# A vision block's last stage: the sum with z moves from VectorE to TensorE

## The reference, cut to what matters

```python
h = _L0_tok_ref(x, ...)
h = h + _L0_attn_ref(_layernorm(h, axis=-1), ...)
h = h + _L0_ffn_ref(_layernorm(h, axis=-1), ...)
...
def _L0_ffn_ref(x, ...):
    ...
    moe_out = jnp.einsum('bseh,bse->bsh', expert_out, sparse)
    return _layer_norm(x + moe_out, gamma, beta)
```

## Time and profile before

| | us |
|---|---|
| median of 3 runs | 2013.91 |
| lowest and highest run | 2012.23, 2017.13 |
| profiled execution: its own time | 2015.43 |
| profiled execution: span | 2013.5 |
| PE busy | 1491.8 (74%) |
| PE weight loads (PEld) | 986.3 (49%) |
| DVE busy | 1425.9 (71%) |
| ACT busy | 1361.4 (68%) |
| POOL busy | 1095.7 (54%) |

### The profile page before, as it was taken

How to read it: one execution, slowest core, us unless ns; L and a number is a source line. 1 busy time by engine, 2 the same in 40 slices (tenths; PEclk the granted TensorE clock), 3 DMA queues, 4 the chain that set the end, 5 groups by cost and what they waited for, 6 DMA issues and landing times. The chain is left out here.

```text
span 2013.5 us, 49200 instructions
## 1 busy us (share of the span) xinstructions
PE 1491.8 (74%) x12152; PEld 986.3 (49%) x12153; DVE 1425.9 (71%) x3598; ACT 1361.4 (68%) x3957; POOL 1095.7 (54%) x1852
## 2 busy tenths in 40 slices
PE   6999957856656565664488885888882999995664
PEld 5999954421111111111244443445441988885563
DVE  2554559977777777786466666788886777675798
ACT  1333324419999999999599995777662776665675
POOL 2333330036666666664355553477775788887454
PEclk9999988965555555555555555555555999998887
DMA  7664410002222222221544543544533555554995
GB/s 297 251 244 175 183 40 1 1 25 81 87 76 85 76 75 76 79 93 55 120 137 137 149 147 116 167 154 152 153 131 111 138 139 142 139 147 115 296 288 155
DMA packets 184973, 263.31 MB, mean 131 GB/s; under 512 B 28372, under 2 KB 147363, under 8 KB 180328
## 3 DMA queue, kind: packets, MB, share of 16 engines
q1 hardware_dynamic: 137456, 202.16, 32.1%
q0 software_dynamic: 19840, 39.17, 5.5%
q10 hardware_dynamic: 27540, 20.52, 3.3%
HBM read 149.17 MB, written 108.01 MB: 128 GB/s over the span
## 5 line engine op out<-in xcount | busy, mean ns | idle before, releaser
L956 ACT ACTIVATE exps_summed<-s,neg_shift 128x197 f32<-128x197 f32 x1184 | 481.9, 535 | 32.1 <-POOL neg_shift L830 30.1
L956 ACT ACTIVATION_READ_ACCUMULATOR exps_summed<-s,neg_shift (+1 forms) x1184 | 339.2, 317 | 0.0
L993 DVE TENSOR_REDUCE score_max<-s 128x788 f32 (+3 forms) x320 | 285.9, 893 | 66.5 <-PE s L900 58.8
L1353 ACT ACTIVATE exps<-st,scalars 128x788 f32<-128x788 f32 (+1 forms) x320 | 246.4, 892 | 17.1 <-PE st L1262 17.1
L2034 POOL DMA_INDIRECT expert_sums<-y_tile,row_places x216 | 218.2, 1010 | 60.5 <-issue 28.6
L384 PE MATMUL mm<-w_tok,x_transposed 128*128 128x192 f32 x1176 | 209.4, 329 | 0.8 <-ACT x_transposed L345 0.8
L345 ACT COPY x_transposed<-tp 128x768 f32<-128x768 f32 x98 | 78.1, 798 | 176.8 <-PE tp L376 176.8
L384 PEld LDWEIGHTS mm<-w_tok,x_transposed 128*128 128x128 f32 x1176 | 190.8, 192 | 1.2 <-ACT x_transposed L345 1.2
L1173 POOL TENSOR_SCALAR probs<-exps 128x788 bf16<-128x788 f32 (+1 forms) x160 | 130.0, 819 | 101.9 <-ACT exps L1353 101.8
L367 POOL TENSOR_SCALAR x_patches<-x_tile 128x768 f32<-128x768 f32 x98 | 81.5, 832 | 187.8 <-PE tp L376 172.1
L900 PE MATMUL s<-k_int,qk_int 16*128 16x197 bf16 x768 | 98.7, 354 | 108.8 <-ACT exps_summed L956 106.0
(11 more groups left out here) (413 smaller groups left out, 4432.8 us busy)
## 6 DMA issues: line engine op xcount, KB each, us to landing
x_tile<-in_x SPq DMA_DIRECT2D x21, 1792.0 KB, 10.9
z_tile<-listed_rows SPq DMA_DIRECT2D x108, 196.0 KB
v_ints<-v_slots SPq DMA_DIRECT2D x32, 480.0 KB
v_slots_in<-v_ints SPq DMA_DIRECT2D x32, 480.0 KB, 3.7
q_ints<-qk_int SPq DMA_DIRECT2D x32, 295.5 KB
k_ints<-k_int SPq DMA_DIRECT2D x32, 295.5 KB
q_shifted<-q_ints SPq DMA_DIRECT2D x32, 295.5 KB, 3.6
k_ones<-k_ints SPq DMA_DIRECT2D x32, 295.5 KB, 4.5
```

Of the source, the lines that this page charges most:

```text
L956: act.activation(gone[:, w % 2, k], ps[(turn + w) % 3][:, k, 0:SEQ], ACT.Exp, scale=alpha, bias=nb[:, s, to:to + 1], accum_out=p.lsum[:, b ...
L993: dve.tensor_reduce(columns(m, u), src, op=ALU.max, axis=AXL.X).then_inc(max_done, 1)
L1353: act.activation(ex[:, v % 4, 0:size(u)], src, ACT.Exp, scale=alpha, bias=p.col(C_LNSA)).then_inc(e_ready, 1)
```

## The change

PE adds `z` itself: per tile a third product, with the identity matrix (f32, 128x128, `p.idf`) as stationary operand and `z` as moving operand, opens the accumulation in PSUM, and the two products with diagonals follow. For that PE waits for `zd` of its block before the first product. DVE's sum and its semaphore `rsum` are gone, as is DVE's wait for `zd`; ACT, which waited for `rsum` of block n-4 before it overwrote a buffer of `z`, waits for `wsum` of that block.

```diff
@@ def tensor(pe):
         def body(n, s, i, nt):
             pe.wait_ge(diag, n + 1)
+            pe.wait_ge(zd, n + 1)
             need(pe, ys, n - 3)
             need_apart(pe, a_in[s], landed(i, nt), tick_t)
             need_apart(pe, b_in[s], landed(i, nt), tick_t)
             for t, rows in tiles(nt):
                 o = pw[s][0:rows, t, 0:D]
-                nc.tensor.matmul(o, dga[0:rows, s % 2, t, 0:rows], ya[0:rows, s, t], start=True, stop=False)
+                nc.tensor.matmul(o, p.idf[0:rows, 0:rows], z[0:rows, s, t], start=True, stop=False)
+                nc.tensor.matmul(o, dga[0:rows, s % 2, t, 0:rows], ya[0:rows, s, t], start=False, stop=False)
                 last = nc.tensor.matmul(o, dgb[0:rows, s % 2, t, 0:rows], yb[0:rows, s, t], start=False, stop=True)
             last.then_inc(wsum, 1)
@@ def scalar(act):
             act.wait_ge(h_in[s], landed(i, nt))
-            need(act, rsum, n - 3)
+            need(act, wsum, n - 3)
@@ def vector(dve):
             dve.wait_ge(wsum, n + 1)
-            dve.wait_ge(zd, n + 1)
-            for tt, rows in spans(nt):
-                ins = dve.tensor_tensor(pw[s][0:rows, tt, 0:D], pw[s][0:rows, tt, 0:D], z[0:rows, s, tt], ALU.add)
-            ins.then_inc(rsum, 1)
-            dve.wait_ge(rsum, n + 1)
             for t, rows in tiles(nt):
                 ins = dve.bn_stats(st6[0:rows, t], pw[s][0:rows, t, 0:D])
```

More of the change, by code:

```diff
@@ L2202, in finish @@
     rs3 = p.sb("rstd3", [128, 2, 4], F32, c)
-    (init, w_in, diag, wsum, rsum, sts, ags, ves, rsd, scaled, based, ys, zd, tick_v, tick_t, tick_p) = p.sems(
-        p.ctx, "i", "init w_in diag wsum rsum sts ags ves rsd scaled based ys zd tick_v tick_t tick_p")
+    (init, w_in, diag, wsum, sts, ags, ves, rsd, scaled, based, ys, zd, tick_v, tick_t, tick_p) = p.sems(
+        p.ctx, "i", "init w_in diag wsum sts ags ves rsd scaled based ys zd tick_v tick_t tick_p")
     h_in = p.sems(p.ctx, "i", "h_in0 h_in1 h_in2 h_in3")
```

## The result

The changed kernel takes 2139.1 us (median of 4 runs, 2135.2 to 2143.4) against 2014.1 before (also the median of 4, one run more than in the table ahead): the ratio is 1.062, with a 95% interval of 1.061 to 1.064. That is 125 us more; 2131 was forecast, in a range of 2117 to 2152.

What follows compares the result with a forecast made beforehand. DVE was taken to bound the last stage at 5.37 us a block. Turns of 10.52 us between PE and ACT would end it at 2123.8 instead of 2006.28, 117.5 us more, giving 2131 us, range 2117 to 2152.

Steps and rivals of the forecast that it cites:

- The ring: Last stage: PE ends a block, ACT makes next diagonals, then z, PE starts; 10.5 us a block instead of 5.37; 88%.
- handover: From the end of ACT's last instruction to PE's first product: 0.40 us taken, between 0.29 and 0.48.
- idle stretch: PE's idle time before each block's burst: 0.01 + 2.35 + 1.85 + 0.40 = 4.61 us.
- The burst: PE's 12 products of a block, begun at 1.2 GHz and ended at 2.4 GHz: 5.9 us, ends 5.6 and 7.1.
- low stretch: Time at 1.2 GHz at the start of each PE burst: 3.6 us, ends 3.0 and 6.0.
- The sum: Block 0, 23 turns of the ring and DVE's last two blocks: last stage ends at 2123.8, 117.5 us later.
- B: Rival: the ring, but PE's clock stays high; 39 us less, 2092 us; 4%.
- C: Rival: the ring, and PE's clock never rises in a burst; 12.6 us a block, 2181 us; 3%.
- D: Rival: z is ready on ACT when PE asks; 1989 us, or 2009 us if DMA is next; 3%.
- DVE branch: D with DVE still the bound: DVE's 24.6 us come off, 1989 us; chance 0.02.
- DMA branch: D with DMA the bound at 305 GB/s, 5.15 us a block: 5.3 us off, 2009 us; chance 0.01.
- E: Rival: z early enough, but PE the bound at its low clock; 8.0 us a block, 2077 us; 2%.

Runs made afterwards that it cites:

- the wait alone: The kernel before with one line added, PE waiting for z of its own block before its 8 products: 2284.9 us against 2171.6, ratio 1.052.
- the product alone: The kernel before with one further identity product per tile on PE and no further wait, DVE still adding z: 2172.0 us against 2171.6, ratio 1.000.
- two edits that open one link: The changed kernel with z ahead of the diagonals on ACT (ratio to before 1.013), or with four buffers of diagonals instead of two (1.030).
- fillers: The changed kernel with 12 more products per block on PE ahead of its wait for z, results overwritten: 2096.9 us against 2014.9 before, ratio 1.039.
- everything open: The changed kernel with z first on ACT, the store one block later and four buffers of diagonals: 2154.0 us against 2177.2 before, ratio 0.989.
- the sum left out: The kernel before without DVE's sum of z, so the output lacks z: 2143.8 us against 2171.6, ratio 0.987.

## Why the prediction was right

**The ring.** It was forecast from the order of the code on ACT and is shown from four sides: the wait alone makes 113 us, the product alone nothing, and each of two edits that open one link takes off 63 to about 99 us. Its terms against the profile: PE's end to ACT 0.01 us forecast, 0.14 in the turns shown; diagonals 2.35 and 2.35; z 1.85 and 1.85; handover 0.40 and 0.50. The idle stretch was forecast at 4.61 us and is 4.60 to 4.96 in the loop, 4.8 in the mean. One sign was named wrongly: the profile was to put this stretch down to ACT's z, and puts it down to DVE's rows or to "issue"; the time lines show z as the link all the same, and with the wait alone the profile names z 16 times.

**The burst.** 5.9 us forecast. From block 1 at 1882.55 us to block 23 at 2119.75 (same time line) 22 turns take 237.2 us, 10.78 us each, so the mean burst is 6.0 us. The products cost the forecast 0.64 and 0.325 us. The low stretch was 3.6 us in the forecast, taken from the middle of three; the turns vary, with bursts from 5.5 to 7.2 us. That the middle of only three bursts came within 0.1 us of the mean of 22 is partly luck. Since the fillers price the clock at 43 us, this was the right thing to put the width of the range on.

**The sum.** From PE's first product to DVE's end the forecast has 255.8 us and the profile 263.1 (1871.34 to 2134.48). Most of the 7.3 us lies in the 22 turns, 237.2 us where the forecast has 22 x 10.52 less 2 x 0.35, 230.7. Of these 6.5 us about 4.2 are the idle stretches (0.2 us each in the loop, PE's end to ACT and the handover) and 2.3 the bursts. 1.2 are block 0's burst (6.9 against 5.6), whose clock did not rise after 3.0 us as before: the window from 1872.0 to 1876.0 is still at 0.50. The end of the stage gives back 0.4. The forecast median was 8 us low.

**The rivals.** B and C (clock always high or always low) did not occur in the changed kernel. Both occur in the experiments, and they are priced: with fillers the ring costs 82 us, where B had 78, and with the wait alone every product is low. D did not occur in the changed kernel either, but it named the right condition, z early enough: the versions that meet it are faster than before. Its DVE branch, 24.6 us, is what happened there (19.5 us, and 23 with everything open; 28 with the sum left out), while its DMA branch is refuted. The 305 GB/s were worked out from a stretch at 290 GB/s whose busy share of 0.95 did not mean that DMA was the limit: the same share rises to 1.10 at 363 GB/s. The prediction could have seen it: the earlier trace rows has 316 to 329 GB/s at shares of 1.01 to 1.07. The Trainium skill (Perfetto Trace Analysis, section Roofline) gives 358 GB/s as a core's share, and more for a core alone. The 351 to 363 GB/s that these runs drew agree with it better than with my estimate. E did not occur: with z ready PE's clock is 1.00 in the middle of the stage (everything open, 2040 to 2120 us).

## What to carry to other kernels

When work moves from one engine to another, list what the new engine must now wait for, and where the producer makes it in its own program; if the producer's preceding step waits for the receiver's preceding block, the two engines run in turns, however little they have to do. The price of such a ring is the sum of its links per turn, and here also TensorE's lower clock after its idle stretches, 43 of the 125 us. The same change is worth 23 us instead of costing 125 if the producer makes the new input first, and no buffer or store closes the ring again; each ring that is opened uncovers the next longer one.

## What the runs showed of the hardware

The share of busy DMA time is no fraction of a limit: it read 0.95 at 290 GB/s and 1.10 at 363 GB/s in the same stage. The changed kernel gained 43 us from 12 useless products a block, since PE at 1.00 does in 4.1 us what takes it 6.0 us otherwise. The granted clock can miss the work altogether: with the wait alone it read 0.50 in the bursts and 1.00 in part of each idle stretch. And of three chips two were 157 and 162 us (8%) slower than the third in the same kernel, ahead of the last stage, while the last stage, with DVE adding z, took 138 to 140 us on each; the cause of that was not looked into.
